# Moving a group's feed-forward products behind the next group's scores, and LayerNorm 2 into the weighted sum, in a causal attention and low-rank FFN layer on eight cores

## The reference

```python
q = x @ Wq;  k = x @ Wk;  v = x @ Wv                  # 1024 x 1024 each
s = q @ k^T / 32, causal
x = layernorm(x + softmax(s) @ v @ Wo)
h = gelu((x @ U1) @ V1 + b1)                          # rank 256, hidden width 4096
x = layernorm(x + (h @ U2) @ V2 + b2)
```

## Time and profile before

| | |
|---|---|
| time, median of 3 runs | 1734.16 us (1698.42 to 1964.55) |
| profiled execution | 1696.7 us, span 1695.2 us |
| span of the eight cores | 1687.4 to 1695.2 us |
| TensorE busy | 1575.7 us, 93% |
| VectorE, ScalarE busy | 674.8 us (40%), 623.6 us (37%) |
| granted TensorE clock, dies 0 and 1 | 0.981 and 0.983 |
| DMA | 242.47 MB, mean 143 GB/s |

### The profile page before, as it was taken

One profiled execution on the slowest core, in us unless ns is written; L12 is line 12 of the kernel. 1 busy time (PEld: TensorE's weight loads), 2 busy tenths in 40 slices (PEclk: granted clock), 3 DMA queues, 4 the chain that ended last, 5 costly groups with the idle time before them and its releaser, 6 DMA issues.

```text
span 1695.2 us, 26259 instructions; the slowest of 8 cores (1687.4 to 1695.2 us)
## 1 busy us (share of the span) xinstructions
PE 1575.7 (93%) x8505; PEld 780.7 (46%) x8672; DVE 674.8 (40%) x1394; ACT 623.6 (37%) x1255; POOL 97.5 (6%) x137
## 2 busy tenths in 40 slices
PE   7888949999999999999999999999999999999985
PEld 2444424445444544454444454444454454454432
DVE  2435244172536251650525521453520535361053
ACT  3532621742355126440264420554420264441033
POOL 0111011010100010100101000110000001000000
PEclk9999979999999999999999999999999999999988
DMA  9899973845646546516755246645246215424301
GB/s 291 261 246 154 123 182 100 100 150 177 121 100 199 171 103 95 197 46 196 177 88 199 101 148 225 78 130 182 96 144 217 99 45 204 150 100 150 124 1 50
DMA packets 72046, 242.47 MB, mean 143 GB/s; under 512 B 4960, under 2 KB 10224, under 8 KB 61296
## 3 DMA queue, kind: packets, MB, share of 16 engines
q1 hardware_dynamic: 60320, 190.86, 33.5%
q0 software_dynamic: 11600, 49.93, 19.9%
HBM read 252.40 MB, written 52.43 MB: 180 GB/s over the span
## 4 chain that ended last, share of the span: by engine, by line
PE 88%; DMA 4%; issue 2%; ACT 2%; DVE 2%; DVEq 1%; SPq 0%; another core or an unknown queue 0%; ACTq 0%
PE ps L620 27%; PE ps L588 26%; PE ps L746 7%; PE ps L738 6%; PE ps L693 6%; PE ps L572 6%; PE ps L604 3%; DMA p_sb<-xtb 2%; PE ps L724 2%; PE ps L772 1%; PE ps L562 1%; DMA wf<-xo 1%; ACT p_sb L879 1%; PE ps L550 1%; DMA wf<-wkt 1%
## 5 line engine op out<-in xcount | busy, mean ns | idle before, releaser
L620 PE MATMUL ps<-p_sb,x_ring 128*128 128x512 bf16 (+3 forms) x2243 | 465.8, 362 | 12.6 <-ACT p_sb L859 4.0
L588 PE MATMUL ps<-x_ring,zt 128*128 128x512 bf16 (+2 forms) x2166 | 445.7, 362 | 2.3 <-ACT zt L782 0.4
L620 PEld LDWEIGHTS ps<-p_sb,x_ring 128*128 128x128 bf16 x2304 | 217.9, 98 | 236.6 <-issue 14.5
L588 PEld LDWEIGHTS ps<-x_ring,zt 128*128 128x128 bf16 x2208 | 211.4, 98 | 228.2 <-issue 0.5
L792 ACT ACTIVATE p_sb<-ps,nm 128x512 bf16<-128x512 f32 (+3 forms) x288 | 187.3, 651 | 283.8 <-DVE nm L917 283.7
L917 DVE TENSOR_REDUCE nm<-ps 128x1 f32<-128x512 f32 (+3 forms) x288 | 184.5, 645 | 214.1 <-PE ps L588 213.1
L894 ACT ACTIVATE p_sb<-ps,b_sb 128x512 bf16<-128x512 f32 x256 | 171.6, 688 | 37.4 <-PE ps L738 36.4
L1033 DVE CAST ot<-ps 128x512 bf16<-128x512 f32 x32 | 22.1, 692 | 344.0 <-PE ps L620 344.0
L746 PE MATMUL ps<-p_sb,wf 128*128 128x512 bf16 x501 | 146.3, 379 | 10.1 <-ACT p_sb L894 9.5
L738 PE MATMUL ps<-p_sb,wf 128*128 128x512 bf16 x502 | 146.3, 379 | 1.2 <-ACT p_sb L782 0.6
L385 POOL TENSOR_TENSOR rstd<-vpe,mhalf 128x1 f32<-128x1 f32 x64 | 47.6, 744 | 1461.6 <-DVE vpe L951 1461.6
(11 more groups left out here) (74 smaller groups left out, 980.0 us busy)
## 6 DMA issues: line engine op xcount, KB each, us to landing
x_ring<-xtb SPq DMA_DIRECT2D x67, 1024.0 KB, 5.7
x_ring<-xnb SPq DMA_DIRECT2D x48, 1024.0 KB, 5.4
x<-xo SPq DMA_DIRECT2D x32, 512.0 KB, 9.1
xnb<-xn POOLq DMA_DIRECT2D x8, 2048.0 KB, 37.8
out<-x POOLq DMA_DIRECT2D x28, 512.0 KB, 7.1
xtb<-xt POOLq DMA_DIRECT2D x12, 1024.0 KB, 22.7
x_ring<-xnb SPq DMA_DIRECT2D x16, 768.0 KB, 4.6
wf<-wvt SPq DMA_DIRECT2D x8, 512.0 KB, 17.7
```

What stands on the lines that cost most here:

```text
L588: mm = t.matmul(ps[b][:, 0:w], zt[:, ec * 512 + j * 128:ec * 512 + (j + 1) * 128], xs[:, off + ec * 512:off + ec * 512 + w], start=(ec == ...
L620: mm = t.matmul(ps[b][:, q0:512], ring[:, off + k * step:off + k * step + 128], P[:, p0 + q0:p0 + 512], start=(c == 0 and k == 0), stop=(c ...
```

## The change

- TensorE has all of S of group g in one piece, then V1, gelu and U2 of group g-1 (`ffn_hidden`), then the first eight transposes of group g, then V2 of g-1 (`ffn_out`), then the other transposes with the weighted sum. U2 follows V1 by four tiles, not three. The last group's V1, U2 and V2 come at the end, alone. ScalarE's gelus and VectorE's copies and additions move with them, and the bank table too.
- `h_sb` lies in `zt`, `p1_sb` in a tensor of its own.
- VectorE does all rescaling of a group ahead of the copies of U2's result and of the transposes.
- LayerNorm 2 of group g-1: pieces 0, 1, 2 behind the copy of e = 1 of the weighted sum of group g, pieces 3, 4, 5 behind that of e = 3, pieces 6 and 7 behind that of e = 5. GpSimd's part (`second_norm`) goes ahead of LayerNorm 1 of group g.
- The own rows of x of groups 1 to 3 are loaded into `xo_sb`, in a part of `P` that is free until group 4: for group 1 behind its S, for groups 2 and 3 behind their score loads. For groups 4 to 7 they still go into `x1`, and SP waits for `d_out` and issues them ahead of the values for e = 6. VectorE waits for `d_out` before it writes `x1`.
- The chunk at `c1` is loaded once WVO is complete; `cast_xn` of groups 0 and 1 come behind LayerNorm 1 of group 0.

```diff
-            cast_xn(0)
-            cast_xn(1)
-
...
+            for gi in range(NG):
+                if gi > 0:
+                    second_norm(gi - 1)
+                for j in range(4):
+                    rstd_of(j, s_mv1, s_rs1, 4 * gi + j + 1)
+                if gi == 0:
+                    cast_xt(4)
+                    cast_xt(5)
+                    for i in range(3):
+                        cast_xn(i)
+                elif gi + 2 < NG:
+                    cast_xt(2 * gi + 4)
+                    cast_xt(2 * gi + 5)
+                    cast_xn(gi + 2)
+            second_norm(NG - 1)
...
             load_scores(1, 2)
+            s.wait_ge(d_ct[1], 16)
+            s.wait_ge(out_of["w_act"], 8)
+            s.wait_ge(out_of["w_dve"], 8)
+            s.dma_start(out=P[:, c1:c1 + 4096], in_=xtb.ap()[1]).then_inc(d_c1, 16)
             for c in range(2, 4):
                 store_turned(c, P[:, xt1 + (c - 2) * 4096:xt1 + (c - 1) * 4096])
-            s.wait_ge(d_ct[1], 16)
-            s.wait_ge(s_acc, ACC[("q2", 0, 1)] + 1)
-            s.dma_start(out=P[:, c1:c1 + 4096], in_=xtb.ap()[1]).then_inc(d_c1, 16)
...
+                if g < 4:
+                    s.wait_ge(out_of["x1"], 8 * g)
+                    load_xo(g, xo_sb)
...
                 for e in range(2, 8):
+                    if e == 6 and g >= 4:
+                        s.wait_ge(d_out, 64 * g)
+                        load_xo(g, x1)
                     for u in range(nu):
                         load_values(g, e, u)
-                load_xo(g)
...
             for g in range(NG):
                 nt = 2 * g + 2
                 if g > 0:
-                    for ti in range(1, nt):
+                    for ti in range(nt):
                         score_tiles(g, ti)
+                    ffn_hidden(g - 1)
                 order = turn_order(g)
                 for c, j in order[:8]:
                     turn_tile(g, c, j)
+                if g > 0:
+                    ffn_out(g - 1)
...
                 for e in range(1, 8, 2):
                     src = tile_full(v, ("av", g, e))
                     v.tensor_copy(ot[:, e * 512:(e + 1) * 512], src[:, :]).then_inc(out_of["ot_dve"], 1)
+                    if g > 0:
+                        for k in {1: (0, 1, 2), 3: (3, 4, 5), 5: (6, 7), 7: ()}[e]:
+                            ln2_piece(g - 1, k)
...
                     v.wait_ge(d_xo, 64 * g)
+                    v.wait_ge(d_out, 64 * g)
```

More of the change, by code:

```diff
@@ L79, in psum_numbers, with turns, hidden, ffn_out @@
     product("w", 0, 8)
+    def turns(g, pairs):
+        for c, j in pairs:
+            put(ring, ring_out, ("t", g, c, j), "turn_dve" if j % 2 == 0 else "turn_act")
+    def hidden(g):
+        for rc in range(2):
+            put(acc, acc_out, ("q2", g, rc), "q2")
+        for fc in range(32):
+            put(ring, ring_out, ("h", g, fc), "gelu")
+    def ffn_out(g):
+        for j in range(4):
+            for h in range(2):
+                put(ring, ring_out, ("f", g, j, h), "r2")
     for g in range(NG):
+        order = turn_order(g)
         if g > 0:
-            scores(g, range(1, 2 * g + 2))
-        for c, j in turn_order(g):
-            put(ring, ring_out, ("t", g, c, j), "turn_dve" if j % 2 == 0 else "turn_act")
+            scores(g, range(2 * g + 2))
+            hidden(g - 1)
+        turns(g, order[:8])
+        if g > 0:
+            ffn_out(g - 1)
+        turns(g, order[8:])
         for e in range(8):
@@ L106, in psum_numbers @@
             z(g + 1, 7)
[L107 to L115, removed]
+    hidden(NG - 1)
+    ffn_out(NG - 1)
     return ring, ring_out, acc, acc_out
@@ L386, in rstd_of, with second_norm @@
                                 mhalf[:, :], ALU.pow).then_inc(s_rs, 1)
[L388 to L394, removed]
+            def second_norm(gi):
                 for j in range(4):
@@ L728, in _ @@
                     z_tile(g + 1, 7)
[L730 to L776, removed]
+            ffn_hidden(NG - 1)
@@ L799, in exps, with gelus @@
                                       AF.Exp, bias=nmf[:, j:j + 1], scale=-1.0).then_inc(s_fac, 1)
+            def gelus(g):
+                if g == 0:
+                    sc.wait_ge(d_v1, 16 * 3)
+                for fc in range(32):
+                    b = tile_full(sc, ("h", g, fc))
+                    if fc >= 8:
+                        sc.wait_ge(s_u2, 31 * g + fc - 7)
+                    sc.activation(h_sb[:, (fc % 8) * 512:(fc % 8 + 1) * 512], b[:, :],
+                                  AF.Gelu_apprx_tanh, bias=b1_sb[:, fc:fc + 1]
+                                  ).then_inc(out_of["gelu"], 1)
             def z_out(g, f):
@@ L851, in _ @@
                 if g > 0:
-                    for ti in range(1, 2 * g + 2):
+                    for ti in range(2 * g + 2):
                         exps(g, ti)
+                    gelus(g - 1)
                 for c, j in turn_order(g):
@@ L887, in _ @@
                     z_out(g + 1, 7)
[L888 to L898, removed]
+            gelus(NG - 1)
         @blk.vector
@@ L1004, in _ @@
                 if g > 0:
-                    pieces = list(range(8))
-                    for ti in range(1, nt):
+                    for ti in range(nt):
                         for j in range(4):
                             row_max(g, ti, j)
-                            if pieces:
-                                ln2_piece(g - 1, pieces.pop(0))
                 order = turn_order(g)
-                for c, j in order[:8]:
+                for c, j in order:
                     rescale(g, c, j)
@@ L1019, in _ @@
                     product_out("w", wvo, 1.0, 0, (7,))
-                for i, (c, j) in enumerate(order):
-                    if i + 8 < len(order):
-                        rescale(g, *order[i + 8])
+                else:
+                    ffn_middle(g - 1)
+                for c, j in order[:8]:
+                    if j % 2 == 0:
+                        turn_out(g, c, j)
+                if g > 0:
+                    ffn_out(g - 1)
+                for c, j in order[8:]:
                     if j % 2 == 0:
@@ L1043, in _ @@
                     v.wait_ge(d_xo, 64 * g)
+                    v.wait_ge(d_out, 64 * g)
+                own = xo_sb if 1 <= g <= 3 else x1
                 for j in range(4):
```

88 lines of the change are left out of this document (70 added, 18 removed).

## The result

The changed kernel is slower: it took 1751.83 us (the profiled execution) and 1753.66 us, against 1698.42 and 1706.12 of the kernel before; ratio 1.0297, 95% interval 1.0194 to 1.0399, so clear of no change, but not quite clear of 2%.

A forecast was written before the change was run, and what follows sets the result against it. TensorE, busy 1575.7 of 1695.2 us, was taken to bound the kernel. From the profiled 1696.7 us, 109 us of new stops less 34 us of gains gave 1772 us; range 1735 to 1820, own range 1754 to 1789.

The forecast's parts named there:

- first rival: Weighted sums, groups 4 to 7: value load not held up by four loads ahead; stops 17.3 us, 1744 us; chance 0.13.
- what it takes: Weighted sums, groups 4 to 7: TensorE stops 24.2 us for e=6 values; with clock 27.2 us, four times, 109 us.
- The store: Link of the stop's chain: a store of group g-1 lands 6 us after GpSimd issues it.
- GpSimd's issues: Link of the stop's chain: first store issued 0.58 us after its norm, the next 1.33 us later.
- The four loads and the value load behind them: End of the stop's chain: issuing four 512 KB loads takes 2.77 us; the value load lands 12.0 us after issue.
- The clock: TensorE behind each stop in groups 4 to 7: granted clock at 0.50 costs 3 us more.
- The gains: Whole kernel: earlier chunk load and rescaling, less the gelu loss, save 34 us, bounds 26 and 41.
- (a): Group 1's fourth score chunk: issued earlier, its load is hidden; stop and slow clock gone, gain 21.3 us.
- (b): Rescaling before the transposes: done during V1 and U2, it saves 18 of 23.6 us, bounds 13 and 22.
- (c): First gelu before U2: stop 1.9 us instead of 1.2, seven times; 5 us lost, bounds 2 and 8.
- The second: More stops, from group 0's late stores, V2's additions or late rescaling: 10 to 30 us extra, about 1792 us; chance 0.15.
- third rival: Groups 4 to 7: stores complete before SP comes to its wait, so no stop; 1663 us; chance 0.04.

The follow-up runs named there:

- e3: Changed kernel with the four own-row loads of x behind the values for e = 6, SP's wait still ahead of them; 1728.56 us.
- e2: Changed kernel with LayerNorm 2's last two norms moved from behind the copy of e = 5 to behind e = 3; 1689.72 to 1691.2 us.
- e5: Kernel before with only the early load of group 1's fourth score chunk, issued once WVO is complete; 1679.63 to 1684.26 us, ratio 0.9902.
- e6: e1 with VectorE's rescaling late again, after U2's copies and between the transposes' copies; 1683.95 to 1689.35 us, ratio 0.9928 to before.
- e10: e1 with U2 five tiles behind V1 instead of four, timed beside a repeat of e1; 1655.49 to 1660.75 us, ratio 0.9773 to before.
- e1: Changed kernel with SP's wait and the own-row loads of groups 4 to 7 back behind all value loads; 1663.95 to 1666.15 us, ratio 0.9808.
- e8: e1 with the casts of groups 0 and 1 issued ahead of LayerNorm 1 of group 0, as before; 1667.78 us.

## Why the prediction was right, and what was off

**The number**: the direction and the mechanism were right, but 1751.8 us lies 20 us below the forecast and just under its own range of 1754 to 1789. It is nearer to the first rival's 1744, so the time alone would have spoken for that rival; the trace of the stops and e3 decide against it.

**What bounds the kernel, and the sum's shape**: right. TensorE's idle time is what moved, in both directions, and each stop forecast was there, in groups 4 to 7 and in no other.

**The stop (step "what it takes")**: the mechanism was right in every link, the size too large: 24.2 us forecast, 20.3 measured on average on the slowest core (the longest stop of each of the eight cores is 17.7 to 21.1 us). Two terms were mis-sized. The store: 6 us taken, between the least and the median of transfers that came four in a row and had loads beside them; as the second of two, with SP standing still, it was 4.4 (772.47 to 776.89). In e2, where four come in a row while SP stands still, it took 6.5 (the last of them, issued by 762.67), so the number in a row counts, and not only the loads. GpSimd's issues: 1.33 us apart taken, from four stores in a row; 0.73 measured. With them the chain from e = 5 full to SP's first issue is 7.2 us, where 9.4 was forecast. The four loads and the value load behind them were nearly right (14.8 forecast, 13.7 in group 4). No link came in that the forecast didn't have.

**The clock**: 3 us a stop forecast, 7.4 us in all measured, 1.9 each. The one stop from which it was read was followed by some 6 us of slow work, these four by 3 to 4. With both, 109 us was forecast and 88.5 came.

**The gains**: 34 forecast, 33 measured. (a) 21.3 forecast; the stop and its slow clock are gone, and alone the edit brings 17 (e5), as the clock is low in more places then. (b) 18 forecast out of 23.6, 20 measured (e6, and the 3.6 us of waits left). (c) -5 forecast; the wait grew from 9.5 to 13.8 us, 4.3, and two slow stretches of about 2 us each behind it, which no step had. One small wait is new besides, which no step had: 2.3 us in group 3 for a score chunk whose load ran beside a cast (1.3 to 5.2 in the experiments with the new order, none in e10). The parts add up near enough, 21 + 20 - 4 - 4, but with the 17 of e5 they don't: that the sum of the gains came out within 1 us is luck in part.

**The rivals**: the first (the queue costs nothing) falls with e3, which prices the queue at 7 us a stop. The second (further stops) didn't come, but for the 2.3 us in group 3: no value load is late in groups 1 to 3, and V2's additions hold up nothing. The 0.4 us a group that are left at the transposes stand ahead of V2, at the seventh tile, whose bank waits for a copy that VectorE makes behind its two copies of U2's result. The third rival's condition didn't come, since SP stood at the wait in all four groups; its time without stops, 1663 us, is what e1 measured with the loads behind (1664 to 1666).

**What was not foreseen**: that a faster kernel was one move away. The order of the feed-forward work is sound; the stops that outweighed its gain, 88.5 us, came out of where one wait and four loads stand in SP's list. With that undone and one more tile between V1 and U2, the kernel takes 0.9773 of the time before.

## What to carry to other kernels

A wait in the queue that issues loads is paid by whatever load stands behind it, not by the one that needs it; before you put one there, ask what the queue was ahead by, and whether the event it waits for can come at all before that lead is used up. Price it as chain less cover: the links from the event to the landing of the next load that the compute engine wants, less the work it still holds. To fill a wait of one engine with another stage, check what the helpers do meanwhile: here the gain was VectorE's rescaling in the time of V1 and U2, and without that the same order gave none of it. And loads that a new order issues earlier can come to run beside other transfers than before: look at what is in flight when they are issued.

## What the runs showed of the hardware

- A wait of 2.0 us, with TensorE busy before and behind it, was followed in some groups by some 3.5 us at a granted clock of 0.50 and in most by none (18 of 168 on the eight cores of three runs); at 1.5 us none of 112 was, on the eight cores of two. Where it happens, the wait costs about twice its length. Several short waits close together were followed by it too: 1.50, 0.84 and 1.18 us within 5 us, before the slow stretch at 386 us of the kernel before.
- One MB behind 2 MB on the same queue landed in 11.1 us, as the first of the queue, with 2 MB behind it, in 6.8. A 512 KB store landed in 2.9 us at the least and 3.9 in the median in the changed kernel, where they go out in pairs; 7.1 in the median before, four in a row and with loads beside them.
- Loads that SP issued while a casting transfer of 2 MB from GpSimd had been in flight for 16 us or more landed about when it had (0.2 us ahead of it to 2.3 us behind it): the load of group 1's fourth chunk took 38.5 us, the changed kernel's first loads beside five such casts 20.5 to 27.3 us. Issued within 2 us of such a cast (e8) the same load took 12.4 us, with none beside it (e1) 10.7.
